# A graph network on one core: one comparison instead of two makes the one-hots of an adjacency unit

## The reference

```python
h = jnp.maximum(_layernorm(x, axis=-1), 0.0)
# twice (layers 0 and 1): mean over the incoming edges, two products, relu
agg = jax.ops.segment_sum(h[src], dst, N) / jnp.maximum(cnt, 1.0)[:, None]
h = jax.nn.relu(agg @ W_l + h @ W_r + b)
x = x + h
h = jnp.maximum(_layernorm(x, axis=-1), 0.0)
# third layer: a message for each edge, summed at its source
m = jax.nn.relu(jnp.concatenate([h[src], h[dst]], axis=-1) @ W_interact + b_interact)
m_i = jax.ops.segment_sum(m, src, N) / 4.0
out = x + h + jax.nn.relu((h + m_i) @ W_update + b_update)
```

## Time and profile before

| | us |
|---|---|
| median of 3 runs | 1517.28 (1516.06 to 1519.37) |
| the profiled execution | 1513.23 |
| its span, first to last instruction | 1511.4 |
| first comparison to last build of the first layer | 125.7 to 520.6 |
| VectorE busy in the span | 1307.1 |
| TensorE busy in the span | 1318.1 |

### The profile page before, as it was taken

One profiled execution on the slowest core, in us unless ns is written; L12 is line 12 of the kernel. 1 busy time (PEld: TensorE's weight loads), 2 busy tenths in 40 slices (PEclk: granted clock), 3 DMA queues, 4 the chain that ended last, 5 costly groups with the idle time before them and its releaser, 6 DMA issues.

```text
span 1511.4 us, 40749 instructions
## 1 busy us (share of the span) xinstructions
PE 1318.1 (87%) x15612; PEld 1129.9 (75%) x15612; DVE 1307.1 (86%) x3899; ACT 939.7 (62%) x1831; POOL 922.8 (61%) x942
## 2 busy tenths in 40 slices
PE   1425989999999998999999679999999999999987
PEld 1213767777777766777777678898999999998987
DVE  7938899999999646677676779999999999999998
ACT  2645788878778730010000558888888888888886
POOL 5263408888781006777760167777777777777773
PEclk7755999999999999999999789999999999999999
DMA  3004536464646258999995134444444444444442
GB/s 124 0 1 137 212 133 252 159 254 154 259 158 231 76 158 280 299 308 301 297 297 183 43 96 123 123 130 131 129 133 127 122 142 123 131 124 129 129 121 65
DMA packets 121788, 241.71 MB, mean 160 GB/s; under 512 B 20184, under 2 KB 74601, under 8 KB 121594
## 3 DMA queue, kind: packets, MB, share of 16 engines
q1 hardware_dynamic: 95179, 187.74, 36.8%
q0 software_dynamic: 24832, 50.78, 13.3%
q10 hardware_dynamic: 1584, 0.59, 0.1%
HBM read 169.09 MB, written 73.14 MB: 160 GB/s over the span
## 4 chain that ended last, share of the span: by engine, by line
DVE 38%; PE 35%; ACT 12%; issue 10%; DMA 2%; SPq 1%; POOL 1%; ACTq 0%; DVEq 0%; POOLq 0%
PE ps L1271 13%; DVE room L2211 7%; ACT lnw L1132 6%; PE ps L1253 6%; DVE hot L1834 5%; PE ps L1242 4%; PE ps L1477 3%; DVE ps L2247 3%; DVE hot L2201 2%; DVE hot L1829 2%; DVE slab L2253 2%; PE ps L1311 2%; DVE keys L1960 2%; DVE keys L1959 2%; ACT slab L1153 1%
## 5 line engine op out<-in xcount | busy, mean ns | idle before, releaser
L1021 ACT ACTIVATE slab<-ps 128x980 f16<-128x980 f32 x256 | 321.5, 1277 | 93.0 <-PE ps L1242 85.5
L932 POOL DMA_INDIRECT cells<-b_rows,work x236 | 239.7, 1016 | 74.8 <-issue 68.9
L1477 PE MATMUL ps<-slab,room 125*128 125x128 f16 x3538 | 235.8, 220 | 34.2 <-DVE room L2211 31.7
L1253 PE MATMUL ps<-slab,room 128*128 128x320 f16 x1568 | 251.9, 300 | 0.1
L1132 ACT ACTIVATE lnw<-iota_w,keys 128x126 f32<-128x126 f32 x750 | 242.4, 389 | 0.0
L1477 PEld LDWEIGHTS ps<-slab,room 125*128 125x128 f16 x3538 | 206.5, 98 | 47.4 <-DVE room L2211 47.3
L1468 PE MATMUL ps<-inv,hot 125*128 125x128 f16 x1800 | 223.8, 220 | 4.9 <-DVE hot L2201 4.9
L1271 PE MATMUL ps<-slab,room 128*128 128x320 f16 x1568 | 227.0, 301 | 0.0
L896 POOL DMA_INDIRECT hot<-t_rows,pairs x160 | 166.0, 1038 | 54.8 <-issue 48.2
L1271 PEld LDWEIGHTS ps<-slab,room 128*128 128x128 f16 x1568 | 153.4, 98 | 59.5 <-issue 2.7
L1242 PE MATMUL ps<-hot 128*128 128x245 bf16 x1024 | 160.8, 282 | 36.5 <-DVE hot L1834 31.7
(11 more groups left out here) (373 smaller groups left out, 2392.4 us busy)
## 6 DMA issues: line engine op xcount, KB each, us to landing
slabs_d<-slab SPq DMA_DIRECT2D x14, 3920.0 KB, 13.3
slab<-slabs_d SPq DMA_DIRECT2D x98, 560.0 KB, 5.2
hot<-lane_d SPq DMA_DIRECT2D x50, 576.0 KB
inv<-inv_row SPq DMA_DIRECT2D x32, 160.0 KB, 7.6
keys<-up_d SPq DMA_DIRECT2D x25, 160.0 KB
room<-up_d SPq DMA_DIRECT2D x25, 160.0 KB
cells<-b_rows,work POOLq DMA_INDIRECT x236
t_rows<-room SPq DMA_DIRECT2D x1, 3200.0 KB, 12.8
```

The costliest lines, as they stand in the source:

```text
L932: p.indirect_dma_start(rows_g[gi % RS][:, j, :], None, b_rows, bass.IndirectOffsetOnAxis(ap=node_t[:, t:t + 1], axis=0)).then_inc(e_gath[g ...
L1021: a.activation(slab[par][:, :, u * UB * BW:(u + 1) * UB * BW].rearrange("p h (k d) -> p k h d", k=UB), psum_unit(u).rearrange("p k (h d) - ...
L1253: last = t.matmul(ps[:, 4 + s % 2, 0:SC], table[:, h, term, :], slab[s % 2][:, h, :], start=k == 0, stop=k == HI * HALVES - 1)
L1477: last = t.matmul(to, end_hot[g // 3][0:BN, u:u + P], bt[0:BN, bt_at(tile, w), k, :], start=False, stop=w == w1 - 1 and k == HALVES - 1)
```

## The change

One comparison makes the one-hots of all 4 bins of a unit. Each bin takes three parts of 128 columns in the buffer: the low one-hot, columns 0 to 127 of the high one, and columns 128 to 255 of it. So that one row of numbers 0..127 can serve all three, `decode` keeps three numbers for each bin, each written twice: low, high, and high - 128. They lie in the unused third of `room` (`cell_parts`). A unit's result is 4 x 3 x 128 = 1536 numbers, in one instruction. In a build the stationary operand is now contiguous (it had a step of four), and the moving operand is as it was. `decode(1)` is cut to the 384 columns that the first layer still needs. The tile `iota_lo` is dropped, with the GpSimd instruction that filled it; `hot` grows from 4 x 1496 to 4 x 1536 columns.

```diff
-        hot = sb("hot", [P, 4, (P + HB + 1) * UB], bf16)
-        iota_lo = sb("iota_lo", [P, P, UB], bf16)
+        hot = sb("hot", [P, 4, UB * PARTS * P], bf16)
...
+        spare = room_b[:, NT * HALVES * P:NT * TERMS * P]
+        cell_parts = spare[:, 0:NU * UB * PARTS * 2].rearrange("p (c a e) -> p c a e", a=PARTS, e=2)
...
-            numbers(iota_lo[:, :, :], [[1, P], [0, UB]])
...
-                lo = hot[:, u % 4, 0:P * UB].rearrange("p (w k) -> p w k", k=UB)
-                hi = hot[:, u % 4, P * UB:(P + HB + 1) * UB].rearrange("p (k w) -> p k w", k=UB)
+                made = hot[:, u % 4, :].rearrange("p (k w) -> p k w", k=UB)
                 to = psum_unit(u)
                 for k in range(UB):
-                    last = t.matmul(to[:, k, :], lo[:, :, k], hi[:, k, 0:HB], start=True, stop=True)
+                    last = t.matmul(to[:, k, :], made[:, k, 0:P], made[:, k, P:P + HB], start=True, stop=True)
...
-                twice = [P, KH, 2]
-                chain(v.scalar_tensor_tensor(out=cell_hi[:, part, :], in0=dec_i[:, 0, :].unsqueeze(2).to_broadcast(twice),
-                                             scalar=float(BW), in1=dec_i[:, 2, :].unsqueeze(2).to_broadcast(twice),
+                n = min(h * KH + KH, NU * UB) - h * KH
+                to = cell_parts[:, h * KH:h * KH + n, :, :]
+                twice = [P, n, 2]
+                chain(v.scalar_tensor_tensor(out=to[:, :, 1, :], in0=dec_i[:, 0, 0:n].unsqueeze(2).to_broadcast(twice),
+                                             scalar=float(BW), in1=dec_i[:, 2, 0:n].unsqueeze(2).to_broadcast(twice),
                                              op0=ALU.mult, op1=ALU.add))
-                chain(v.tensor_scalar(dec_i[:, 0, :], dec_i[:, 1, :], P - 1, None, ALU.bitwise_and))
-                chain(v.tensor_copy(cell_lo[:, part], dec_i[:, 0, :]))
+                chain(v.tensor_scalar(to[:, :, 2, :], to[:, :, 1, :], -float(P), None, ALU.add))
+                chain(v.tensor_scalar(dec_i[:, 0, 0:n], dec_i[:, 1, 0:n], P - 1, None, ALU.bitwise_and))
+                chain(v.tensor_copy(to[:, :, 0, :], dec_i[:, 0, 0:n].unsqueeze(2).to_broadcast(twice)))
...
-                v.tensor_tensor(out=hot[:, u % 4, 0:P * UB].rearrange("p (w k) -> p w k", k=UB),
-                                in0=iota_lo[:, :, :],
-                                in1=cell_lo[:, bass.ds(b, UB)].unsqueeze(1).to_broadcast([P, P, UB]),
-                                op=ALU.is_equal)
-                both = [P, UB, (HB + 1) // 2, 2]
-                v.tensor_tensor(out=hot[:, u % 4, P * UB:(P + HB + 1) * UB].rearrange("p (k w t) -> p k w t", k=UB, t=2),
-                                in0=iota_hi[:, :].rearrange("p (w t) -> p w t", t=2).unsqueeze(1).to_broadcast(both),
-                                in1=cell_hi[:, b:b + UB, :].unsqueeze(2).to_broadcast(both),
+                both = [P, UB * PARTS, P // 2, 2]
+                v.tensor_tensor(out=hot[:, u % 4, :].rearrange("p (a w e) -> p a w e", a=UB * PARTS, e=2),
+                                in0=iota_hi[:, 0:P].rearrange("p (w e) -> p w e", e=2).unsqueeze(1).to_broadcast(both),
+                                in1=cell_parts[:, b:b + UB, :, :].rearrange("p c a e -> p (c a) e").unsqueeze(2
+                                                                                       ).to_broadcast(both),
                                 op=ALU.is_equal).then_inc(A["hot"], 1)
```

More of the change, by code:

```diff
@@ L64, in gnn_kernel @@
     HALVES = 2
+    PARTS = 3
     LIFT = 4096.0
@@ L296, in gnn_kernel @@
         table = room_b.bitcast(f16)[:, 0:NT * HALVES * P].rearrange("p (t k n) -> p t k n", k=HALVES, n=P)
+        spare = room_b[:, NT * HALVES * P:NT * TERMS * P]
+        cell_parts = spare[:, 0:NU * UB * PARTS * 2].rearrange("p (c a e) -> p c a e", a=PARTS, e=2)
+        assert NU * UB * PARTS * 2 <= NT * (TERMS - HALVES) * P and HB <= 2 * P and 16 * GE <= NT * HALVES * P
         dst_r = table_f[0:HG, 0:2 * GE].rearrange("p (h e) -> p h e", h=2).bitcast(i32)
```

## The result

The changed kernel takes 1523.8 us (median of 20 runs, 1517.2 to 1530.2), the kernel before 1517.7 beside it (20 runs). The ratio is 1.0039 (1.0022 to 1.0055): 6.1 us slower, where 5.3 us faster was forecast, and outside the range. The profiled execution of after is 1522.73 us with a span of 1520.9, against 1513.23 and 1511.4.

What follows compares the result with a forecast made beforehand. VectorE was taken to set the pace in the first layer's middle, TensorE at its end. Comparison -5.0, builds -1.5 and decode +1.2 summed to -5.3 us, from the median 1517.28 to 1512.0, range 1507.5 to 1518.

Steps and rivals of the forecast that it cites:

- The comparison: First layer, VectorE: one 950 ns instruction holding the engine 868 ns replaces two, gaining 47 ns a unit; 5.0 us taken.
- rival (3): Merged comparison runs at half rate, lasting 1.75 us: 157 us slower, 1674 us; chance 0.08.
- the second rival: The dropped comparison instruction's whole duration comes back, 131 ns a unit, giving 1501.7 us; chance 0.08.
- The builds: TensorE's first-layer builds: contiguous stationary loads save up to 5 ns each, 20 ns a unit; 1.5 us taken.
- The decode: VectorE ahead of the first comparison: added subtraction and larger copy in decode(0) cost 1.2 us, bounds 0.5 and 2.5.
- The sum: Whole kernel: -5.0 - 1.5 + 1.2 = -5.3 us; first comparison to last build becomes 388 to 389 us.
- At nothing go: GpSimd ...: Items priced at zero: GpSimd's dropped number generator, which ran long before the first unit, the moved buffers and the clock.
- The reserve: TensorE's 20.8 us of waiting for the comparison, said to be four times the gain that draws on it.
- Rival (1): TensorE takes over in the middle window, VectorE's tail-add waits growing over 2 us: -1.3 us, 1516.0; chance 0.21.
- The prediction's last sentence: If the first layer gains 6 us but the time doesn't, something omitted waits behind it, such as a slab store or gather.
- I see nothing that gives it back.: Behind the first layer: what follows starts earlier by as much, so the 5.3 us gain is kept.

Runs made afterwards that it cites:

- x9: The changed kernel unaltered, run once more for a second trace: 1521.83 us, one run.
- x10: The kernel before unaltered, run once more for a second trace: 1512.19 us, one run.
- x5: The changed kernel without 140 of the 160 gathers of the first layer's tail: 1509.21 us, ratio 0.9963.
- x6: The kernel before without the same 140 of 160 first-layer gathers: 1514.31 us, ratio 1.0012.
- x1: The changed kernel with its comparison split into two instructions (512 low, 984 high results): 1516.92 us, ratio 1.0006.
- x4: The changed kernel with its comparison cut into two instructions of 768 results, two bins each: 1518.62 us, ratio 1.0024.
- x3: The kernel before with the first tail group 12 units earlier, the last where it was: 1512.34 us, ratio 0.9985.
- x7: The changed kernel with one comparison for two units (3072 results): 1543.0 us, ratio 1.0194.
- x11: The changed kernel with a tiny VectorE instruction of one SBUF input behind each comparison: 1537.6 us, ratio 1.0127.
- x8: The changed kernel with three comparisons of 512 results for each unit: 1556.58 us, ratio 1.0284.

## Why the prediction was wrong, point by point

**The comparison: right.** 950 ns and a hold of 868 were forecast; 954 at the median and 868 were measured, so rival (3) is out, and the second rival with it: the next start comes 0.08 us before the end here too. The prediction gave the rule of the Trainium skill ("VectorE: DVE Perf Modes", section "The DRAIN you can't avoid") without its exception: that section adds that a next operation which is not held starts earlier. These starts are such a case, and do not speak against the page.

```profile
L1835 DVE TENSOR_TENSOR hot<-iota_hi,room 128x1536 bf16<-128x1536 bf16 x256 | 234.1, 955 | 6.7 <-PE ps L1244 5.6
```

**The builds: right.** Loads at 98 ns and builds 0.105 us apart (four from 419.50 to 419.92), with 98 and 0.104 to 0.105 forecast:

```profile
L1244 PEld LDWEIGHTS ps<-hot x1024: 95/98/152, 129.0 to 526.1; 128*128 128x128 bf16 x171
...
419.50 0.58 PE L1244 MATMUL ps<-hot 128*128 128x245 bf16 x4
419.92 0.98 PE L1255 MATMUL ps<-slab,room 128*128 128x320 f16 x6
```

**The decode: nearly right.** From the start of the high number to the first comparison 4.25 us against 3.28: +0.97, with 1.2 forecast. The subtraction took 0.59 (0.85 taken, 0.49 to 1.49 as bounds), the copy 0.83 (0.85). decode(1) takes 5.01 us in place of 5.14, with 0 forecast. The runs of two results with gaps cost nothing that can be seen: L1764 takes 1.49 us as L1760 did. The estimate by the Trainium skill ("Vector Engine (DVE) Microarchitecture Reference", section 5.2) did not come true here; that section's figures are for streams of four-byte words. The other 1.2 us of the later first comparison lie ahead of the changed part and vary (it is at 126.0 us in x9, 126.6 in x10).

**The sum: right in the stretch that it counts.** There -5.0 and -1.5 were forecast, and x5's stretch is 6.2 us below that of x6. The two terms are told apart only roughly: x1, with the new layout but two instructions, has 392.0 us, 1.2 below x6 and 2.9 below before, and x5 is another 5.0 below x1. That the medians of x5 and x6 differ by so nearly the 5.3 of the forecast is in part luck, since the intervals of the two ratios leave some 3 us open, and the two profiles show 4.0 us behind the last build that the sum does not have.

**The failed step: "At nothing go: GpSimd ..."** It priced GpSimd by the one instruction that was dropped. The change adds nothing to GpSimd and moves nothing; it lengthens what GpSimd's gathers wait behind. Every VectorE instruction was weighed for its own time, and none for the time in which others can't get past it. The gathers of after are 0.17 us longer on average, their lead is gone by the fifth tail, and TensorE stands for 11.1 us, 9.0 of them for late gathers. The trace of before could have shown the step, but no row of its gathers was read: they are longer than 0.94 us where VectorE's instructions are in the way (three from 306.9 us on below), 160 of them run in the first layer, and the hold that they meet grows from 0.335 and 0.580 to 0.868 us.

```profile
306.90 1.04 POOL L896 DMA_INDIRECT tslot<-t_rows,pairs  x1 [0.30 <-issue]
308.25 1.19 POOL L896 DMA_INDIRECT tslot<-t_rows,pairs  x1 [0.30 <-issue]
309.75 1.14 POOL L896 DMA_INDIRECT tslot<-t_rows,pairs  x1 [0.30 <-issue]
```

**The reserve.** "The reserve is four times the gain" took TensorE's 20.8 us for the only one. There were two, and the other, the lead of the gathers, was down to 4.4 us at its lowest. That view, last issue to first product, was not read. The prediction's last sentence named "a gather" as what might wait, and gave it no price and no chance.

**Rival (1)** had the sign to look for (the waits of L1804 for L1319 over 2 us longer, and they are 13.5) but the wrong mechanism: TensorE is not full, it stands.

**"I see nothing that gives it back."** Behind the last build the changed kernel takes 994.4 us in both profiles, the one before 990.9 and 990.1. The single comparison and the first layer's gathers aren't the reason: x1 takes 994.4, x4 994.1 and x5 995.7. One place is seen, in the second layer: TensorE's wait ahead of the tail's product there is 2.27 us before (749.13) and 4.46 after (756.10), the latter behind a gather of 3.14. The rest is open; x3, built on the kernel before, takes 993.8 as well, and x7 only 988.9.

## What to carry to other kernels

Before two VectorE instructions are merged, ask who needs a gap between them: GpSimd's indirect DMAs waited for the running instruction's end here, and a longer hold cost 0.17 us in each gather without a change on GpSimd. Measure the slack of each producer by its lead (last issue to first use), not by the busy share; here 4 to 13 us of lead decided over some 11 us of stalls. Where a faster engine eats the lead, try an earlier consumer: the tail's sums free the twenty buffers that the gathers fill, so earlier tails, spread over more units, let the gathers start earlier, and that alone turned +0.39% into -0.54%.

## What the runs showed of the hardware that was not expected

- A gather takes 0.942 us alone; if it starts in a VectorE instruction with two SBUF inputs and gets through at its handover, it ends 0.90 us behind that. Beside an instruction with one input in PSUM 116 of 123 took 0.940 to 0.948 us.
- A gather that misses one handover in a row of such instructions misses the others too (827 of 827), and took up to 8.6 us (x3, at 209.2); an instruction of two numbers behind each comparison kept all at 2.98 us or less. What decides the first handover (703 of 851 went through) is not known.
- The rows are there 1.6 us behind the last issue as a rule, and later beside a store. Of the 25 stalls of over 0.7 us in all these runs, 15 end 1.6 to 1.7 us behind the tail's last gather; the other ten end 3.7 to 6.6 us behind it. In nine of the ten a slab's store of 3.9 MB (11 to 16 us long) had begun 2.7 to 12.4 us before that gather's end, in the tenth (x11 at 476.6) 0.4 us before; in all of the 15 it had either begun at most 0.3 us before or 14 us and more. So 2.1 of the 11.1 us of stalls in after, and a part of the largest ones of x3, x8 and x11 (10.9, 10.9 and 7.2 us), aren't GpSimd's hold. That the store holds the rows back was not tested.
